# The opening of a transformer kernel: who issues the first query transfers, and in which order the work of tiles 0 and 1 stands

## The reference

```python
x = x + tanh(g_xattn[0]) * diff_attention(ctx, layernorm(x), Wq, Wk, Wv, lambdas)   # 32 half heads of 8
x = x + tanh(g_ffn[0])   * zone_ffn(layernorm(x), W1, b1, W2, b2, Wa, Wb)           # top 3 of 8 zones
x = x + tanh(g_xattn[1]) * attention(layernorm(x), ctx, Wq, bq, Wo, bo)             # 16 heads of 16
x = x + tanh(g_ffn[1])   * gated_ffn(layernorm(x), w_gate, w_up, w_down)            # int weights / 127
```

```python
q, k, v = dec @ Wq.T, enc @ Wk.T, enc @ Wv.T          # dec = layernorm(x), enc = context
att = softmax(einsum('bhtd,bhnd->bhtn', q, k) * 8 ** -0.5)      # 32 half heads, 77 keys
att = att[:, :, 0] - lam * att[:, :, 1]               # lam from four small vectors
out = einsum('bhtn,bhnd->bhtd', att, v)
```

## Time and profile before

| | |
|---|---|
| time, median of 3 runs | 722.27 us (721.84 to 723.39) |
| the profiled execution: its own time | 724.65 us |
| the profiled execution: its span | 722.8 us |
| PE busy | 641.1 us (89%) |
| DVE busy | 368.1 us (51%) |
| ACT busy | 370.6 us (51%) |
| POOL busy | 114.3 us (16%) |

### The profile page before, as it was taken

How to read it: one execution, slowest core, us unless ns; L and a number is a source line. 1 busy time by engine, 2 the same in 40 slices (tenths; PEclk the granted TensorE clock), 3 DMA queues, 4 the chain that set the end, 5 groups by cost and what they waited for, 6 DMA issues and landing times.

```text
span 722.8 us, 10171 instructions
## 1 busy us (share of the span) xinstructions
PE 641.1 (89%) x3676; PEld 487.8 (67%) x3676; DVE 368.1 (51%) x814; ACT 370.6 (51%) x627; POOL 114.3 (16%) x158
## 2 busy tenths in 40 slices
PE   2377798888889999999999999999888879999996
PEld 2354455545448788888888777787566657888885
DVE  6447566586575352534536535434446655443332
ACT  4124465655666574646657535545753655333332
POOL 8000434334462000000000000000021313000000
PEclk9757899998779999999999999999888878999999
DMA  7301111023003021030203240000161100000000
GB/s 221 87 3 44 46 47 47 18 65 100 3 29 117 2 79 38 0 117 1 89 29 89 64 141 2 1 1 2 26 197 42 47 2 2 0 30 1 29 30 29
DMA packets 22737, 34.66 MB, mean 48 GB/s; under 512 B 4640, under 2 KB 13216, under 8 KB 22688
## 3 DMA queue, kind: packets, MB, share of 16 engines
q1 hardware_dynamic: 21376, 32.87, 15.1%
q10 hardware_dynamic: 864, 0.86, 0.5%
q0 software_dynamic: 448, 0.29, 0.4%
HBM read 18.93 MB, written 2.10 MB: 29 GB/s over the span
## 4 chain that ended last, share of the span: by engine, by line
PE 74%; DVE 8%; ACT 5%; SPq 4%; issue 3%; DMA 3%; POOL 2%; ACTq 1%; DVEq 0%; POOLq 0%
PE SC L1127 27%; PE PV L1127 25%; PE PV L1145 5%; PE SC L1258 4%; PE AUX L1127 4%; PE AUX L1230 3%; DVE NM L1011 3%; SPq L521 2%; SPq L532 2%; DMA QG<-NMT 2%; PE AUX L1186 2%; ACT XN L729 1%; DVE O L1019 1%; ACTq L712 1%; ACT NMT L770 1%
## 5 line engine op out<-in xcount | busy, mean ns | idle before, releaser
L871 DVE TENSOR_TENSOR HL<-HF,HH 128x512 fp32r<-128x512 f32 x120 | 83.3, 695 | 156.2 <-ACT HH L823 156.0
L781 ACT ACTIVATE PB<-SC 77x1024 f32<-77x1024 f32 x96 | 95.1, 1014 | 63.7 <-PE SC L1258 63.3
L823 ACT ACTIVATE HH<-PV 128x512 fp32r<-128x512 f32 x96 | 57.3, 597 | 66.7 <-PE SC L1127 66.7
L1258 PE MATMUL SC<-QG,KA 128*128 128x512 f32 x192 | 75.2, 487 | 16.0 <-DMA QG<-NMT 14.0
L818 ACT ACTIVATE HF<-PV 128x512 f32<-128x512 f32 x96 | 57.5, 599 | 58.4 <-PE PV L1127 56.3
L1127 PE MATMUL PV<-XH,WAH 128*128 128x512 f32 x192 | 78.2, 407 | 1.0 <-DVE O L1019 1.0
L1127 PE MATMUL PV<-XL,WAH 128*128 128x512 f32 x192 | 76.4, 398 | 0.0
L1127 PE MATMUL PV<-XH,WAL 128*128 128x512 f32 x192 | 76.2, 397 | 0.0
L1127 PE MATMUL SC<-HL,WBH 128*128 128x512 f32 x192 | 75.6, 394 | 0.0
L1127 PE MATMUL SC<-HH,WBH 128*128 128x512 f32 x192 | 75.3, 392 | 0.0
L1127 PE MATMUL SC<-HH,WBL 128*128 128x512 f32 x192 | 75.0, 390 | 0.0
(11 more groups left out here) (236 smaller groups left out, 1190.8 us busy)
## 6 DMA issues: line engine op xcount, KB each, us to landing
QG<-QH SPq DMA_DIRECT2D x120, 64.0 KB, 2.0
WSA<-in_wa SPq DMA_DIRECT2D x6, 1024.0 KB, 4.9
WSB<-in_wb SPq DMA_DIRECT2D x12, 512.0 KB, 6.8
QG<-QL SPq DMA_DIRECT2D x60, 64.0 KB, 2.0
X<-in_x SPq DMA_DIRECT2D x4, 512.0 KB, 6.0
out_x<-X SPq DMA_DIRECT2D x4, 512.0 KB, 2.6
WI<-in_wg SPq DMA_DIRECT2D x1, 768.0 KB, 4.4
WI<-in_wu SPq DMA_DIRECT2D x1, 768.0 KB, 6.8
```

Of the source, the lines that this page charges most:

```text
L781: act.activation(probs(n)[0:S, :, :], SC[0:S, n % 2, :, :], ACT.Exp, scale=SCALE[a]).then_inc(exp_done, 1)
L823: act.activation(HH[s % 2][:, :], PV[:, s % 2, :], ACT.Gelu_apprx_tanh).then_inc(act_done, 1)
L871: return dve.tensor_tensor(dst, raw, hi.bitcast(F32), ALU.subtract)
L1258: ins = pe.matmul(SC[:, n % 2, i, :], KALL[a][:, at_h:at_h + P], QG[m % 2][:, h // NS[a], :], start=True, stop=True)
```

## The change

Four things change. The half of tile 0's query transfers that ScalarE issued goes to GpSimd, and the same split is now made for tile 1 (r = 0, 1 on SP, r = 2, 3 on GpSimd); GpSimd's transfers have semaphores of their own, `first_moved`, and who needs the regrouped query waits for both. In the list, `norm` of tile 1 stands ahead of the later keys. The first six maxima of tile 0 stand between the scaling and the transposes of tile 1, and the coefficients and the values' keys behind the other ten. The opening ends with the transfers of tile 1's first half and ten maxima of tile 0's second half; only six of these are left for the gaps of units 0 to 2, their `negmax` and tile 1's second transfers follow unit 3, and `heads` of batch 1 follows unit 12.

```diff
@@ plan
     steps = norm(ATT0, 0) + [("weights_split", 1), ("weights_split", 0), ("scale", ATT0, 0), ("turn", ATT0, 0)]
-    steps += keys(0, 0, 1) + [("query", 0, 0)] + moves(0, 0) + keys(0, 1, 5) + [("heads", 0, 0)]
-    steps += norm(ATT0, 1) + [("scale", ATT0, 1), ("turn", ATT0, 1)]
-    steps += maxima(0, 0, 0) + [("negmax", 0, 0, 0), ("query", 0, 1), ("coefficients",), ("heads", 0, 1)]
+    steps += keys(0, 0, 1) + [("query", 0, 0)] + moves(0, 0) + norm(ATT0, 1) + keys(0, 1, 3) + [("heads", 0, 0)]
+    first, second = maxima(0, 0, 0), maxima(0, 0, 1)
+    steps += [("scale", ATT0, 1)] + first[:6] + [("turn", ATT0, 1)] + first[6:] + [("coefficients",)] + keys(0, 3, 5)
+    steps += [("negmax", 0, 0, 0), ("query", 0, 1), ("q_move", 0, 1, 0)] + second[:10]
     left = []
     for j in range(J):
         side = {}
-        fillers = [(maxima(0, j, 1), 0, 5)]
-        side.setdefault(5, []).append(("negmax", 0, j, 1))
+        fillers = [(maxima(0, j, 1), 0, 5) if j else (second[10:], 0, 3)]
+        side.setdefault(5 if j else 3, []).append(("negmax", 0, j, 1))
         if j + 1 < J:
             fillers.append((maxima(0, j + 1, 0), 6, 13))
             side.setdefault(13, []).append(("negmax", 0, j + 1, 0))
+            side.setdefault(6 if j else 3, []).append(("q_move", 0, j + 1, 1))
             if j == 0:
-                side.setdefault(1, []).append(("q_move", 0, 1, 0))
-            side.setdefault(6, []).append(("q_move", 0, j + 1, 1))
+                side.setdefault(12, []).append(("heads", 0, 1))
@@ semaphores and helper
+        first_moved = [[sem(f"first_moved{i}{c}") for c in range(KC)] for i in range(2)]
...
+        def query_moved(eng, n, c):
+
+            eng.wait_ge(q_moved[n % 2][c], 16 * (6 + 12 * (n // 2)))
+            if n < 2:
+                eng.wait_ge(first_moved[n][c], 16 * 6)
@@ SP, q_move
-                    for r in range(2 if n == 0 else 4):
+                    for r in range(2 if n < 2 else 4):
@@ GpSimd
+                elif kind == "q_move" and J * step[1] + step[2] < 2:
+
+                    _, a, j, c = step
+                    used(pool, ("query", a, j, c))
+                    for r in range(2, 4):
+                        for q, src in enumerate((QH, QL, QH)):
+                            pool.dma_start(QG[j][32 * q:32 * q + 32, 4 * c + r, :].bitcast(F32),
+                                           src[32 * r:32 * r + 32, c, :].bitcast(F32)).then_inc(first_moved[j][c], 16)
@@ ScalarE
-                elif kind == "q_move" and step[1:3] == (0, 0):
-
-                    c = step[3]
-                    act.wait_ge(qh_ready, c + 1)
-                    used(act, ("query", 0, 0, c))
-                    for r in range(2, 4):
-                        for q, src in enumerate((QH, QL, QH)):
-                            act.dma_start(QG[0][32 * q:32 * q + 32, 4 * c + r, :].bitcast(F32),
-                                          src[32 * r:32 * r + 32, c, :].bitcast(F32)).then_inc(q_moved[0][c], 16)
...
-                            act.wait_ge(q_moved[(n - 1) % 2][c], 16 * 12 * ((n - 1) // 2 + 1))
+                            query_moved(act, n - 1, c)
@@ TensorE, max
-                        pe.wait_ge(q_moved[n % 2][u // half], 16 * 12 * (n // 2 + 1))
+                        query_moved(pe, n, u // half)
```

## The result

The changed kernel takes 702.70 us (median of 4 runs, 702.37 to 704.13) beside 722.83 us for the kernel before: ratio 0.972, interval 0.9691 to 0.9749. Run again on another chip it took 705.05 us (six runs) beside 723.65: 0.9752, 0.9715 to 0.979. The forecast was 710.0 with 706 to 717.5: the kernel got faster by the path that the forecast named, but by more than its range allows. The part on why it was right or wrong says which terms were too small.

A forecast was written before the change was run, and what follows sets the result against it. The prediction took a chain of waits in the opening, first ScalarE's DMA issues, as the bound. 4.5 us at first scores grew to 12.3 at u=8, all kept: 722.27 median to 710.0 us, range 706 to 717.5.

The forecast's parts named there:

- Step 1: Opening: transfers move from ScalarE to GpSimd at 0.54 us an issue; tile 1's scaling ends at 30.1, 8.9 us earlier.
- Step 2: Opening: six maxima fill VectorE's wait for scaling; the other ten start at 33.5 and end at 37.5, before 48.80.
- Step 3: Opening: coefficients and values' keys go between; turned maxima start 9.3 us earlier, at 39.6; query product through QL keeps 7.4 us.
- Step 4: End of opening: ten second-half maxima add 3.3 us before the first scores, which start at 50.3, a gain of 4.5 us.
- Step 5, first half: Tile 0 up to u=8: with work gone from it, scores u=8 come at 62.4 instead of 74.68, 12.3 us earlier.
- Step 5, second half: From u=8 to tile 1's first scores: 21.3 us before, order unchanged except heads of batch 1, which are hidden.
- the 5.0: Tile 0, from turned maxima c=1 to scores u=8: evacuation, four issues and landing take 5.0 us.
- Nothing given back: Behind tile 1's first scores: the 12.3 us won by there stay whole to the end.
- Rival A: Opening: GpSimd's queue is the bound, rsqrt through ten maxima late by 1.8 to 6.6 us; 712 to 717; chance 0.17.
- B: Tile 0 takes the gain back: only first scores move (4.5 us), u=8 at 66 or later; 714 to 718; chance 0.18.
- C: Opening: GpSimd's transfers ahead of tile 1's rsqrt cost over 1.6 us each; gain gone at 1.56; chance 0.05.
- D: Opening: ScalarE's issues weren't the cause, only the order gains, 3 to 6 us; 716 to 719; chance 0.07.

The follow-up runs named there:

- b1: Changed kernel with tile 1's statistics and rsqrt ahead of the first keys, scaling right behind QH, transposes ahead of all sixteen maxima; 704.7 us, ratio 0.9713.
- g1: Changed kernel with six further transfers of the same shape on GpSimd's queue ahead of tile 1's rsqrt; 708.9 us in one run.
- c1: The kernel before, executed again unchanged for its stage lengths; 723.0 us.
- e3: Changed kernel with all sixteen maxima of tile 0's second half inside tile 0, turned after unit 5, none early; 708.3 us, ratio 0.9819.
- e2: Changed kernel's list of steps with the transfers as before (ScalarE issues half of tile 0's, SP all of tile 1's); 709.2 us, ratio 0.9822.

## Why the prediction was right or wrong, by its steps

By means of the traces (before three, after four) the span fell 18.7 us, from 722.5 to 703.8. Beside it stands the pair of traces of the first measurement.

```
                          forecast   measured, means   first pair
opening to first scores      4.5        6.3               5.3
first scores to u=8          7.8        8.1               9.2
u=8 to tile 1                0          2.9               0.8
behind tile 1                0          1.4               6.4
sum                         12.3       18.7              21.7
```

Up to tile 1 the forecast is 5.1 us short by the means: 2.9 between u=8 and tile 1, 1.8 in the opening, 0.3 between. The first medians differ by 20.1 us, 7.8 more than forecast; what goes beyond the 5.1 lies behind tile 1 and is not traced to the change.

- **Step 1** was right in each part. The issues took 0.51 us instead of 0.54, the rsqrt followed them directly, GpSimd was the last to be ready. The rule of the Trainium skill ("SBUF — State Buffer", section "SBUF: two separate sides"), that GpSimd writes no descriptors while VectorE holds the ports they share, was put at up to 1.8 us. In the trace after, two issues from 25.50 took 1.26 us where pairs had 0.98, and the rsqrt 1.19 where b1 and g1 had 1.04, both beside VectorE's head copies: 0.4 us together, and issues at 26.76 and 27.24 in the middle of these copies took 0.50 each. The trace agrees with a small part of it at most.
- **Step 2** was right: six maxima filled the wait for the scaling (the rest began at 34.62, 33.5 forecast; SP's first issue was 1.1 us later in this trace too).
- **Step 3** had a term too large: turned maxima and query product to the end of QL 7.4 us, where the trace has 5.9 (40.56 to 46.47). The clock rises in the middle of the product: its matmuls go from 0.63 to 0.39 us. Before, this rise came at its end, or in c1 in its middle. Ahead of it the value products now keep TensorE busy without a break; that they bring the rise forward is likely, and no run tests it. The turned maxima themselves start 19.2 us behind SP's issue, 19.4 forecast.
- **Step 4**: 3.0 us for 3.3. That the ten would not hide behind a transfer, only change places, is what e3 shows.
- **Step 5**, first half: 10.75 us for 12.1, against a stretch of before that was 19.9 in my trace and 18.9 in the mean. The plan was right; that the gain came out at 8.1 for 7.8 is in part luck, as two errors of 1 us or more cancel.
- **Step 5**, second half, is the step that failed: "From u=8 to the first scores of tile 1 it was 21.3 us ... Its order doesn't change". The order did not, the wait in front of it did. I had that wait in the rows (1.65 us) and had priced it as 1.65 us, already inside the 5.0. With it TensorE's clock is lower through what follows; the 21.3 of one trace was the short end of 21.3 to 24.5. Without it the stretch takes 20.5 us, so the term put at 0 measured 2.9 us in the means (23.4 to 20.5).
- **"Nothing given back", and nothing more won, behind tile 1**: held in the mean to 1.4 us. What the first pair of traces showed there, 6.4 us, was mostly chance of the clock in the second attention. The 1.4 left isn't settled: with a spread of 5 us and seven traces it can't be told from none.
- **Rival A** named a real path (g1), but an issue costs 0.51 us and the head copies 0.4 in all. **B** had its stall and its lower clock (0.50 from 51 to 53 us), but u=8 came at 60.2 and not 66: over tile 0 as a whole the clock gave more, not less. **C** was far off, as issues cost a third of its point. **D** was right that the order carries most (e2: 13.9 of 17.5 us) and wrong that ScalarE's issues cost nothing: moving them alone is worth 6.3 us of tile 1's start, and 3.5 on top of the new order.

## What to carry to other kernels

A wait of TensorE costs more than its length if it lets the clock drop (here 1.6 us of wait, and 0.8 to 4 us more in the stretch behind it): price it with the stretch behind it at both levels. Before a sum is made, take stage lengths from more than one execution; a stage whose granted clock stands between the two levels has no single length. And when one engine's queue is blocked by issues, ask first which work of other engines can be put beside them: here the order won 14 of 17.5 us and moving the issues 3.5 more. Traces are compared from an event that both kernels reach by the same steps: from the start of the span these 3.5 us looked like 2.4.

## What the hardware showed that was not expected

- GpSimd issued 64 KB transfers inside the core's memory mostly at 0.49 to 0.50 us each, less than SP (0.59 to 0.63) and ScalarE (0.61), and they landed as fast: 2.3 us median beside 2.5 for SP's in the same stretch.
- The second attention took between 87.74 and 93.66 us over twenty traces with the same matmuls (791 or 792 in each stretch), at a mean clock of 0.86 to 0.78, while the gated stage, at 0.99 in the two traces where it was read, took 117.14 to 117.22 in all of them.
- In the kernels whose steps are the same up to there, the first query transfer was issued anywhere from 19.77 to 21.46 us.
